# Four small moves and a new masked maximum in a transformer layer kernel: attention, soft mixture of experts, attention, soft mixture of experts

## The chip, the cores and the metric

The kernel runs on one core of one Trainium2 chip. The metric is device time in microseconds (us). The engines are TensorE (PE, with its weight loads as PEld), VectorE (DVE), ScalarE (ACT), GpSimd (POOL) and SyncE (SP, whose queue issues most DMAs). They run side by side and wait for one another by semaphores.

## What is computed

x has 4096 tokens of 256 numbers. It passes through four layers, each adding to x what it computes from the normalised x:

```python
x = x + attn_a(layernorm(x))     # 16 heads of 16, causal, denom = sum(exp) + exp(denom_bias)
x = x + ffn(layernorm(x))        # soft mixture of 64 experts with 32 slots each
x = x + attn_b(layernorm(x))     # 16 heads of 16, causal softmax
x = x + ffn(layernorm(x))        # the same weights again

# attention
sim = einsum('bhid,bhjd->bhij', q, k) / sqrt(16)
sim = where(j > i, -big, sim)
p = exp(sim - max_j(sim));  out = (p / sum(p)) @ v;  return out @ Wo.T

# mixture
logits = (x @ phi_w.T + phi_b).reshape(t, z, 64, 32)
D = softmax(logits, axis=slots);  C = softmax(logits, axis=experts)
X = D^T x;  X = tanh(layernorm(clip(X)));  Y = X @ expert_w + expert_b;  return C Y
```

## The kernel before, in words

The program is a row of stages, each with its own semaphores and a barrier of all engines at its end (`phase_of`): set-up, then for each of the two halves norm and projection (`norm_and_project`), attention, `project_out_and_norm`, `dispatch`, and `experts_and_combine`. The tags are set, a_qkv, a_att, f_in, f_disp, f_mix, b_qkv, b_att, g_in, g_disp, g_mix. A stage begins when the last engine of the one before has come to the barrier, so a DMA that SP waits for at the end of a stage holds up all engines.

**Set-up.** SP issues the loads of four weights and of x (eight groups), waits for GpSimd's memsets and selects, and then issues five copies: `x_rows` to DRAM (L150) and the turned halves of the mask and of the identity (L154). It waits for all of them at the stage's end (L155, L156).

**Norm and projection.** In layer a VectorE also folds and scales phi, the dispatch weights, in `area`. SP stores its high and low part to `phi_parts` in DRAM (L335) and waits for both stores. `project_out_and_norm` of each mixture loads phi from there.

**Attention.** Heads go in four quads of four. A unit is a quad and a group g of 512 queries; quads 0 and 2 take the groups upwards, quads 1 and 3 downwards, so there are 32 units a layer. Each unit first needs the row maxima of its scores, then the exponentials. For the maxima TensorE makes score items: one item is a pair of heads, one tile of 128 queries and one block c of up to 512 keys (`score`, L742). The two heads' matmuls use different rows of the array (r = 0 and 64) and different banks of PSUM. Where the block is the diagonal one (c == g) its width is 128, 256, 384 or 512 and its last 128 columns lie on the diagonal. There TensorE adds -3.0e38 above the diagonal with two further matmuls per head (L746, L747), each of 64 rows and 128 columns. VectorE takes both heads of an item in one reduction (L889). The ring of items holds two. The exponentials' scores are made the other way round, keys on partitions (`scores_t`, L778): four tiles a step, ScalarE's exp (L846) on each, then the products with V (`p_v`, L797). Which items are made behind which tile is a list worked out in advance (`ring_schedule`): the maxima run about a unit ahead of the exponentials, and behind tiles 1 and 3 of a step one item may stand, head 1 first and head 0 one tile on. In the descending quads the items become fewer towards the end.

**Dispatch.** 64 units (32 tiles of 128 tokens for each half of the slots). For each unit TensorE makes logits (L1105, 12 matmuls), VectorE two maxima and a subtraction (L1207 to L1212), ScalarE the exp, VectorE the sums and reciprocals, GpSimd the quotient d (L1185), ScalarE its high part (L1152), GpSimd its low part (L1189), and TensorE three tiles later the products with the tokens (L1117, 24 matmuls), gathered in four banks. In the second half, after every eighth tile, VectorE merges the two halves' maxima (L1219) and GpSimd cuts them into three bf16 parts (`cut_maxima`, four operations, L1173 to L1179); TensorE turns these three tiles later (L1126) and ScalarE keeps them (L1163). At the half and at the end ScalarE copies the four banks to xacc (L1157).

## Time and profile before

| | |
|---|---|
| Median of 3 runs | 4777.9 us (4777.64 to 4795.27) |
| The profiled execution | 4784.3 us, span 4782.5 us, mean granted TensorE clock 0.971 |
| TensorE busy | 4441.6 us, 93% |
| VectorE busy | 4075.7 us, 85% |
| ScalarE busy | 3132.5 us, 65% |
| GpSimd busy | 1211.5 us, 25% |
| Attention a from its first maximum to its last | 142.3 to 1506 us |

Times in the rows below are from the span's start. A busy share is an average over stages. In a timeline row the first number is the start, the second the length, and the brackets give how long the engine was idle before it and who released it. Rows of one shape are merged, and the number behind x is how many they hold. Matmuls are pipelined and their ends are modelled, so the length of a group of them is a little longer than the time it takes from the next.

### The profile page before, as it was taken

To read this page: it belongs to the slowest core of one execution; us is meant where nothing else is said; L and a number is where in the kernel's file an instruction comes from. 1 tells how busy PE (TensorE), PEld (TensorE's weight loads), DVE (VectorE), ACT (ScalarE), POOL (GpSimd) and SP (SyncE) were. 2 spreads that over 40 slices of the span, in tenths; PEclk is the share of its full clock that TensorE was granted. 3 is DMA by queue.
4 is the path that set the end of the run, shared out by engine and by line. 5 is a ranking of instruction groups with operands and counts; after the bars stand their busy time and mean duration, and the time that the engine had idled before them with its cause. 6 is when DMAs were issued, how large, how long until landed. Compare 5 with 4: busy or idle time off the path is not lost. (4 is left out here: it accounts for less than half of the span.)

```text
span 4782.5 us, 97694 instructions
## 1 busy us (share of the span) xinstructions
PE 4441.6 (93%) x40558; PEld 1955.9 (41%) x40558; DVE 4075.7 (85%) x4651; ACT 3132.5 (65%) x5879; POOL 1211.5 (25%) x1201
## 2 busy tenths in 40 slices
PE   7799999999998899899997999999999998998998
PEld 4222223222224566456662222232222345664666
DVE  5899998999885898678848999989998868885887
ACT  3378988889997444334344789888899974443443
POOL 1100001100002576445301000011000015774543
PEclk9799999999999899999997999999999999999999
DMA  6100000000000000310040000000000000004000
GB/s 183 54 21 2 2 15 15 14 14 4 2 2 23 1 1 1 107 36 0 0 126 26 17 2 2 22 9 15 15 2 2 2 22 1 1 1 142 10 13 13
DMA packets 73767, 112.29 MB, mean 23 GB/s; under 512 B 12501, under 2 KB 56789, under 8 KB 69077
## 3 DMA queue, kind: packets, MB, share of 16 engines
q1 hardware_dynamic: 68746, 99.96, 6.3%
q0 software_dynamic: 4608, 6.50, 1.0%
q8 instruction: 299, 4.90, 0.4%
q14 instruction: 114, 0.93, 0.1%
HBM read 73.70 MB, written 31.47 MB: 22 GB/s over the span
## 5 line engine op out<-in xcount | busy, mean ns | idle before, releaser
L889 DVE TENSOR_REDUCE b_att_mx<-ps 128x2 f32<-128x1024 f32 (+3 forms) x1152 | 1228.4, 1130 | 105.9 <-PE ps L742 80.6
L889 DVE TENSOR_REDUCE a_att_mx<-ps 128x2 f32<-128x1024 f32 (+3 forms) x1152 | 1227.9, 1130 | 102.3 <-PE ps L742 77.7
L846 ACT ACTIVATE b_att_pt<-ps 128x512 f32<-128x512 f32 (+3 forms) x2304 | 1146.9, 560 | 208.7 <-PE ps L778 179.0
L846 ACT ACTIVATE a_att_pt<-ps 128x512 f32<-128x512 f32 (+3 forms) x2304 | 1146.9, 560 | 207.2 <-PE ps L778 177.3
L797 PE MATMUL ps<-b_att_pt,b_v 128*17 128x256 f32 (+1 forms) x8704 | 672.6, 381 | 10.7 <-ACT b_att_osb L833 9.8
L797 PE MATMUL ps<-a_att_pt,a_v 128*17 128x256 f32 (+1 forms) x8704 | 670.5, 380 | 10.7 <-ACT a_att_osb L833 9.7
L723 POOL TENSOR_SCALAR_AFFINE_SELECT b_att_pt<-b_att_pt 128x512 f32<-128x512 f32 x128 | 81.4, 636 | 1122.9 <-ACT b_att_pt L846 1110.6
L723 POOL TENSOR_SCALAR_AFFINE_SELECT a_att_pt<-a_att_pt 128x512 f32<-128x512 f32 x128 | 81.4, 636 | 1120.4 <-ACT a_att_pt L846 1108.1
L778 PE MATMUL ps<-b_q,b_k 51*128 51x512 f16 (+3 forms) x1152 | 363.2, 370 | 0.2 <-ACT b_att_pt L846 0.2
L778 PE MATMUL ps<-a_q,a_k 51*128 51x512 f16 (+3 forms) x1152 | 361.3, 368 | 0.2 <-ACT a_att_pt L846 0.2
L742 PE MATMUL ps<-a_k,a_q 48*128 48x512 f16 (+3 forms) x1152 | 293.9, 379 | 51.9 <-DVE a_att_mx L889 37.9
L778 PE MATMUL ps<-b_att_q,b_att_k 51*128 51x512 f16 (+3 forms) x1152 | 338.7, 365 | 1.1 <-ACT b_att_pt L846 0.6
L778 PE MATMUL ps<-a_att_q,a_att_k 51*128 51x512 f16 (+3 forms) x1152 | 338.4, 365 | 1.0 <-ACT a_att_pt L846 0.6
L742 PE MATMUL ps<-b_k,b_q 48*128 48x512 f16 (+3 forms) x1152 | 298.0, 382 | 41.4 <-DVE b_att_mx L889 33.2
L742 PE MATMUL ps<-b_att_k,b_att_q 48*128 48x512 f16 (+3 forms) x1152 | 320.4, 365 | 5.1 <-DVE b_att_mx L889 4.8
L742 PE MATMUL ps<-a_att_k,a_att_q 48*128 48x512 f16 (+3 forms) x1152 | 320.3, 365 | 5.1 <-DVE a_att_mx L889 4.8
L1152 ACT CAST area<-area 128x1024 f16<-128x1024 f32 x128 | 133.8, 1045 | 287.7 <-POOL area L1185 287.7
L1189 POOL TENSOR_TENSOR area<-area 128x1024 f16<-128x1024 f32 x128 | 272.7, 2131 | 146.1 <-ACT area L1152 145.5
L797 PEld LDWEIGHTS ps<-b_att_pt,b_v 128*17 128x17 f32 x8704 | 145.2, 95 | 356.6 <-ACT b_att_pt L846 211.1
L797 PEld LDWEIGHTS ps<-a_att_pt,a_v 128*17 128x17 f32 x8704 | 145.1, 95 | 356.2 <-ACT a_att_pt L846 210.6
L1117 PE MATMUL ps<-f_xtok,area 128*128 128x256 f16 x1536 | 189.9, 283 | 26.5 <-POOL area L1189 22.7
L1117 PE MATMUL ps<-g_xtok,area 128*128 128x256 f16 x1536 | 190.2, 283 | 25.9 <-POOL area L1189 22.0
(319 smaller groups left out, 7241.0 us busy)
## 6 DMA issues: line engine op xcount, KB each, us to landing
f_mix_ct<-in_expert_w SPq DMA_DIRECT2D x64, 256.0 KB, 4.2
g_mix_ct<-in_expert_w SPq DMA_DIRECT2D x64, 256.0 KB, 4.3
a_parts_q<-a_qkv_cut SPq DMA_DIRECT2D x24, 256.0 KB
a_parts_k<-a_qkv_cut SPq DMA_DIRECT2D x24, 256.0 KB
b_parts_q<-b_qkv_cut SPq DMA_DIRECT2D x24, 256.0 KB
b_parts_k<-b_qkv_cut SPq DMA_DIRECT2D x24, 256.0 KB
x<-in_x SPq DMA_DIRECT2D x8, 512.0 KB, 8.6
out<-x SPq DMA_DIRECT2D x8, 512.0 KB, 2.9
```

Of the source, the lines that this page charges most:

```text
L723: pool.affine_select(out=block_p, in_=block_p, pattern=[[0, 4], [1, P]], compare_op=ALU.is_ge, fill=0.0, base=0, channel_multiplier=-1).th ...
L742: mm = pe.matmul(ps[:, at:at + width], q[quad % 2][h // 2][r:r + ROWS, t0:t0 + P], k[quad % 2][h // 2][r:r + ROWS, c * BANK:c * BANK + wid ...
L778: pe.matmul(ps[:, at:at + width], k[quad % 2][h // 2][r:r + ROWS_M, kb * P:(kb + 1) * P], q[quad % 2][h // 2][r:r + ROWS_M, (g + 1) * BANK ...
L797: mm = pe.matmul(OUT[32 * h:32 * h + VW, lo:hi], v[:, kb, 4 * quad + h, :], pt[:, s % PT_RING, h, lo - left:hi - left], start=(first and h ...
L846: act.activation(pt[:, s % PT_RING, i, 0:width], ps[:, at:at + width], ACT.Exp, scale=unscale).then_inc(pt_ready, 1)
L889: dve.tensor_reduce(mx[u % 2][:, h:h + 2, t, c], both, AX.X, ALU.max).then_inc(ring_read, 1)
L1117: mm = pe.matmul(ps[:, at:at + D], disp[:, n % DISP, dp, eb * P:(eb + 1) * P], xtok[:, t, xp, :], start=(t == 0 and i == 0 and eb % 2 == 0 ...
L1152: act.copy(disp[:, v % DISP, 0, :], ex[:, v % EX, :]).then_inc(high, 1)
L1189: pool.tensor_tensor(disp[:, n % DISP, 1, :], ex[:, n % EX, :], disp[:, n % DISP, 0, :], ALU.subtract).then_inc(d_ready, 1)
```

## The change

It has four parts.

1. Set-up: the five copies move from SP to the end of GpSimd's queue. SP still waits for them.
2. phi's stores: the projection of layer a no longer waits for them. Their semaphore is now kept for the whole kernel, and both mixtures wait for it before they load phi.
3. Dispatch: the four cutting operations no longer stand together between d and its low part, but one each behind the low parts of four tiles (all four behind the last tile for the last chunk). The turn comes six tiles after the chunk instead of three. The copies of the product banks each wait for their own bank (`xa_bank`) instead of for all.
4. Attention: for the diagonal items of quads 1 and 3 with g below 7 (`is_late`) the mask matmuls are left out. VectorE instead makes one `tensor_tensor_reduce` per head that adds a mask tile and takes the running maximum; the sum goes to a scrap tile. Before it VectorE waits until the previous such item is done. The mask tile is made by a memset and a copy at the start of the stage.

```diff
@@ set_up
-            sp.wait_ge(row_made, 2)
-            sp.dma_start(x_rows, ones_row[:, :, :]).then_inc(stored, 16)
-            sp.wait_ge(built, 2)
-            for turned, straight in ((m.mask_turned, m.mask_qk), (m.identb_turned, m.identb)):
-                for r in (0, P // 2):
-                    sp.dma_start(turned[r:r + P // 2, :], straight[P // 2 - r:P - r, :]).then_inc(turned_halves, 16)
             sp.wait_ge(turned_halves, 64)
             sp.wait_ge(stored, 16)
...
             pool.wait_ge(built, n)
+            pool.wait_ge(row_made, 2)
+            pool.dma_start(x_rows, ones_row[:, :, :]).then_inc(stored, 16)
+            for turned, straight in ((m.mask_turned, m.mask_qk), (m.identb_turned, m.identb)):
+                for r in (0, P // 2):
+                    pool.dma_start(turned[r:r + P // 2, :], straight[P // 2 - r:P - r, :]).then_inc(turned_halves, 16)
@@ norm_and_project
-                    sp.dma_start(early.phi_parts[part], parts[:, part, :, :]).then_inc(phi_stored, 16)
-                sp.wait_ge(phi_stored, 32)
+                    sp.dma_start(early.phi_parts[part], parts[:, part, :, :]).then_inc(early.phi_stored, 16)
@@ project_out_and_norm
+            sp.wait_ge(phi_stored, 32)
             for dst, src in loads:
                 sp.dma_start(dst, src).then_inc(loaded, 16)
@@ attention
+def is_late(u):
+
+    return any(UNITS[u][0] == quad and UNITS[u][1] < G - 1 for quad in (1, 3))
...
-                masked_end = c == g
+                masked_end = c == g and not is_late(u)
...
+            dve.memset(mask[:, 0:BANK - P], 0.0).then_inc(mask_made, 1)
+            dve.tensor_copy(mask[:, BANK - P:BANK], m.mask_qk[:, :]).then_inc(mask_made, 1)
+            dve.wait_ge(mask_made, 2)
...
+                if c == g and is_late(u):
+                    wait(dve, ring_read, dumped)
+                    dumped = n + 1
+                    for i in range(2):
+                        last = dve.tensor_tensor_reduce(dump[:, i, 0:width], both[:, i, :], mask[:, BANK - width:BANK], 1.0, NEG,
+                                                        ALU.add, ALU.max, mx[u % 2][:, h + i, t, c:c + 1])
+                    last.then_inc(ring_read, 1)
+                else:
+                    dve.tensor_reduce(mx[u % 2][:, h:h + 2, t, c], both, AX.X, ALU.max).then_inc(ring_read, 1)
@@ dispatch
-    TURN_AFTER = {min(n + 3, UNITS_D - 1 + LAG): j for n, j in CUT_AFTER.items()}
+    PIECES = 4
+    TURN_AFTER = {min(n + PIECES + 2, UNITS_D - 1 + LAG): j for n, j in CUT_AFTER.items()}
+    PIECE_AFTER = {n: [] for n in range(UNITS_D)}
+    for last_tile, j in CUT_AFTER.items():
+        for piece in range(PIECES):
+            PIECE_AFTER[min(last_tile + piece, UNITS_D - 1)].append((j, piece))
...
+                    if t == T - 1 and eb % 2 == 1 and eb + 1 < HALF_EB:
+                        mm.then_inc(xa_bank, 1)
...
-                    act.wait_ge(xa_ready, n - LAG + 1)
                     for b in range(HALF_EB // 2):
+                        if b + 1 < HALF_EB // 2:
+                            act.wait_ge(xa_bank, (HALF_EB // 2 - 1) * half + b + 1)
+                        else:
+                            act.wait_ge(xa_ready, n - LAG + 1)
...
-                if n in CUT_AFTER:
-                    cut_maxima(CUT_AFTER[n])
                 pool.wait_ge(high, n + 1)
                 pool.tensor_tensor(disp[:, n % DISP, 1, :], ex[:, n % EX, :], disp[:, n % DISP, 0, :],
                                    ALU.subtract).then_inc(d_ready, 1)
+                for j, piece in PIECE_AFTER[n]:
+                    cut_piece(j, piece)
```

## Rows read from the trace of the kernel before

**Rows 1.** Table of stretches of attention a: us, busy time of each engine (instructions), clock, DMA.
```profile
546.00:800.00 254.00, 247.54 (x2847) 75.01 (x2847) 239.11 (x252) 227.39 (x450) 17.68 (x49) 1.00 0.04 14
1205.00:1450.00 245.00, 239.08 (x2720) 72.00 (x2717) 210.53 (x213) 225.35 (x453) 15.29 (x38) 1.00 0.01 2
```
**Rows 2.** VectorE's groups by form, 546 to 800 us: busy us, mean ns | idle before.
```profile
L889 DVE TENSOR_REDUCE a_att_mx<-ps 128x2 f32<-128x1024 f32 x180 | 208.8, 1219 | 11.6 <-PE ps L742 10.7
...
L889 DVE TENSOR_REDUCE a_att_mx<-ps 128x2 f32<-128x256 f32 x15 | 6.3, 417 | 0.6 <-PE ps L747 0.6
```
**Rows 3.** VectorE's timeline: a full run of seven; behind a 128-wide and a 256-wide item.
```profile
568.60 8.00 DVE L889 TENSOR_REDUCE a_att_mx<-ps 128x2 f32<-128x1024 f32 x7
...
728.81 4.09 DVE L889 TENSOR_REDUCE a_att_mx<-ps 128x2 f32<-128x1024 f32 x4 [0.40 <-PE ps L742]
733.20 2.36 DVE L889 TENSOR_REDUCE a_att_mx<-ps 128x2 f32<-128x1024 f32 x2 [0.30 <-PE ps L742]
```
**Rows 4.** TensorE's timeline: products of P and V around an unmasked and a masked item.
```profile
1355.19 0.63 PE L797 MATMUL ps<-a_att_pt,a_v 128*17 128x256 f32 x8
...
1356.29 0.63 PE L797 MATMUL ps<-a_att_pt,a_v 128*17 128x256 f32 x8
...
1357.50 0.62 PE L797 MATMUL ps<-a_att_pt,a_v 128*17 128x256 f32 x8
```
**Rows 5.** Who SyncE's queue waited for in set-up: us in total, times, longest.
```profile
SPq L156 <- DMA x_rows<-set_ones_row: 3.7, 1, 3.7
```
**Rows 6.** Timeline of set-up and of GpSimd's first DMAs behind it.
```profile
12.72 0.31 POOL L178 TENSOR_SCALAR_AFFINE_SELECT sameneg<-sameneg 128x128 bf16<-128x128 bf16 x1
13.78 1.24 SPq L154 DMA_DIRECT2D identb_turned<-identb  x2
25.06 2.47 POOL L428 DMA_DIRECT2D a_k<-a_qkv_minus  x4 [0.31 <-POOL a_qkv_minus L425]
```
**Rows 7.** DMA issues: KB each, median us from issue to landing.
```profile
a_k<-a_qkv_minus POOLq DMA_DIRECT2D x4, 24.0 KB, 2.9
```
**Rows 8.** Who SyncE's queue waited for at the end of projection a.
```profile
SPq L73 <- DMA phi_parts<-area: 4.8, 1, 4.8
SPq L338 <- DMA a_parts_k<-a_qkv_cut: 1.7, 1, 1.7
```
**Rows 9.** Timeline there: phi's stores, and the exp of dbias in attention a.
```profile
130.49 1.11 SPq L335 DMA_DIRECT2D phi_parts<-area  x2
...
142.05 0.22 ACT L837 ACTIVATE a_att_dbias<-a_att_dbias 128x16 f32<-128x16 f32 x1 [0.74 <-DMA a_att_dbias<-in_a_db]
```
**Rows 10.** GpSimd's timeline at the first cut of dispatch f.
```profile
1820.29 2.13 POOL L1189 TENSOR_TENSOR area<-area 128x1024 f16<-128x1024 f32 x1 [1.21 <-ACT area L1152]
...
1829.77 1.91 POOL L1185 TENSOR_TENSOR area<-area,f_disp_rds 128x1024 f32<-128x1024 f32 x1
...
1834.07 2.12 POOL L1189 TENSOR_TENSOR area<-area 128x1024 f16<-128x1024 f32 x1
```
**Rows 11.** TensorE's timeline at the first and at the second cut of dispatch f.
```profile
1836.24 2.79 PE L1117 MATMUL ps<-f_xtok,area 128*128 128x256 f16 x24 [0.99 <-POOL area L1189]
...
1876.64 4.46 PE L1117 MATMUL ps<-f_xtok,area 128*128 128x256 f16 x24 [2.00 <-POOL area L1189]
```
**Rows 12.** Timeline at the half (first row) and at the end of dispatch f.
```profile
1792.78 2.05 ACT L1157 ACTIVATE f_xacc<-ps 128x512 f32<-128x512 f32 x4
...
1978.40 2.79 PE L1117 MATMUL ps<-f_xtok,area 128*128 128x256 f16 x24 [1.91 <-POOL area L1189]
...
1981.23 2.06 ACT L1157 ACTIVATE f_xacc<-ps 128x512 f32<-128x512 f32 x4 [6.25 <-PE ps L1117]
```
**Rows 13.** VectorE's groups by form: two inputs at 512 columns, and a very small operation.
```profile
L1010 DVE TENSOR_TENSOR f_xlnT<-ps,f_xlnT 128x512 f16<-128x512 f32 x8 | 5.5, 685 | 0.6 <-ACT f_xlnT L974 0.6
...
L458 DVE SCALAR_TENSOR_TENSOR a_qkv_cut<-ps,qk_scale,a_qkv_cut 128x512 f16<-128x512 f32 x32 | 23.4, 747 | 22.9 <-ACT a_qkv_cut L402 22.9
...
L213 DVE TENSOR_TENSOR qk_unscale<-set_wpower 128x2 f32<-128x2 f32 x1 | 0.1, 129 | 0.0
```

More of the change, by code:

```diff
@@ L632, in attention @@
         den, rden = sb("den", [P, KB, 4]), sb("rden", [P, KB, 4])
+        mask = sb("mask", [P, BANK], BF16)
+        dump = sb("dump", [P, 2, BANK], BF16)
         dbias = sb("dbias", [P, HEADS])
@@ L893, in _, with project_out_and_norm @@
                     dve.tensor_reduce(mfull[u % 2][:, :, :], mx[u % 2][:, :, :, 0:g + 1], AX.X, ALU.max).then_inc(m_full, 1)
[L897 removed]
+def project_out_and_norm(nc, m, ps, tag, attn, wo, bias, w, xlnT, by_token, loads, phi_stored):
     GT = 4
@@ L1167, in _, with cut_piece @@
         def _(pool):
-            def cut_maxima(j):
+            def cut_piece(j, piece):
                 parts = m3[j % 2]
-                pool.wait_ge(mc_made, j + 1)
-                wait(pool, c_turned, j - 1)
-                pool.tensor_copy(parts[:, :, 0, :], mc[:, :, :]).then_inc(c_chain, 1)
-                pool.wait_ge(c_chain, 3 * j + 1)
-                pool.tensor_tensor(mrest[:, :, :], mc[:, :, :], parts[:, :, 0, :], ALU.subtract).then_inc(c_chain, 1)
-                pool.wait_ge(c_chain, 3 * j + 2)
-                pool.tensor_copy(parts[:, :, 1, :], mrest[:, :, :]).then_inc(c_chain, 1)
-                pool.wait_ge(c_chain, 3 * j + 3)
-                pool.tensor_tensor(parts[:, :, 2, :], mrest[:, :, :], parts[:, :, 1, :], ALU.subtract).then_inc(c_cut, 1)
-                pool.wait_ge(c_cut, j + 1)
+                if piece == 0:
+                    pool.wait_ge(mc_made, j + 1)
+                    wait(pool, c_turned, j - 1)
+                    pool.tensor_copy(parts[:, :, 0, :], mc[:, :, :]).then_inc(c_chain, 1)
+                elif piece == 1:
+                    pool.wait_ge(c_chain, 3 * j + 1)
+                    pool.tensor_tensor(mrest[:, :, :], mc[:, :, :], parts[:, :, 0, :], ALU.subtract).then_inc(c_chain, 1)
+                elif piece == 2:
+                    pool.wait_ge(c_chain, 3 * j + 2)
+                    pool.tensor_copy(parts[:, :, 1, :], mrest[:, :, :]).then_inc(c_chain, 1)
+                else:
+                    pool.wait_ge(c_chain, 3 * j + 3)
+                    pool.tensor_tensor(parts[:, :, 2, :], mrest[:, :, :], parts[:, :, 1, :], ALU.subtract).then_inc(c_cut, 1)
             for n in range(UNITS_D):
@@ L1610, in mixture_layer @@
                 with nc.sbuf_tensor(f"{tag}_xtok", [P, T, 2, D], F16) as xtok:
-                    project_out_and_norm(nc, m, ps, f"{tag}_in", m.area, wo, bias, xacc[:, 0:DC, :], xlnT, xtok, loads)
+                    project_out_and_norm(nc, m, ps, f"{tag}_in", m.area, wo, bias, xacc[:, 0:DC, :], xlnT, xtok, loads, early.phi_stored)
                     dispatch(nc, m, ps, f"{tag}_disp", xtok, xlnT, phi, xacc, mct)
```

10 lines of the change are left out of this document (5 added, 5 removed).

## The prediction

> **What bounds the kernel now.** The busy shares (TensorE 93%, VectorE 85%) are averages over unlike stages, so the first view to read is the table of stretches, here for attention layer a [rows 1]. The reader is to see two regimes in it. While quad 1's maxima are made (546 to 800 us) TensorE is busy 247.5 us of 254 and VectorE 239.1: both are at their end, and VectorE has 14.9 us free. From 1205 us on, while quad 3's are made, up to 1450, VectorE has 34.5 us of 245 free, TensorE only 5.9. So the descending run of quad 3 is TensorE's; in quad 1's run the two take turns. The second view is VectorE's maxima by width and then in order of time [rows 2, 3], to price an item and to see where the idle time stands. The third is TensorE's order of work around a masked item [rows 4]. For the set-up and the end of the first projection I read who SyncE waited for and what was issued when [rows 5 to 9], and for the dispatch the order of GpSimd, TensorE and ScalarE around a cut, at the half and at the end [rows 10 to 12].
>
> **Set-up copies on GpSimd's queue.** Five copies leave SP and are issued by GpSimd after its last select. Today they stand on SP behind eight loads of x; the last is issued by 15.0 us (13.78 and 1.24), and SP then waits 3.7 us on x_rows and after it for the turned halves, so the stage ends not before 18.7 [rows 5, 6], and the next begins at 20.3. GpSimd's selects end at 13.03 (12.72 and 0.31); it issues four small DMAs in 2.47 us [rows 6], so five take 3.1, and with the 2.9 us to landing of its copies of minus [rows 7] they land at 19.0, on a queue of their own. SP's now end at about 19.5, as the barrier behind takes 0.8. What is then late is x itself, on whose queue nothing changes. I take -0.8 us, bounds -1.5 and +0.5 (if the two queues share the engines badly). Nothing is queued behind them on GpSimd in that stage. The Trainium skill, "DMA: Bandwidth & Descriptors", section on SWDGE and HWDGE, speaks against it: GpSimd's path has about 1 us to the first byte and SP's about 0.6. By that alone an estimate of the gain is 0.4 us less; no run here has shown the same copy on both.
>
> **phi's stores awaited by the mixture.** SP's last wait of the a projection is 4.8 us on phi_parts [rows 8], after the q and k parts have landed. It goes entirely. What is late next: dbias is the first DMA of attention a, and it is now issued while phi's two megabytes are still on that queue; VectorE's first maximum waits for the exp of dbias, which now runs from 142.05 to 142.27 [rows 9]. phi's issues end at 131.60, and with waits of 1.7 and 4.8 us [rows 8, 9] phi has landed at about 138.2. If dbias lands right behind phi, at 138.5 to 139.3, the exp ends at 138.8 to 139.6: a gain of 2.7 to 3.5 us. If dbias isn't held up, it is 4.8. I take -3.3, bounds -2.5 and -4.8. The new wait stands on SP in front of phi's loads of the mixture, 1.4 ms after the stores landed: nothing, in both layers.
>
> **Masks inside the maxima.** Per attention layer 14 units of quads 1 and 3 have 8 diagonal items each, 112 in all, 28 of each width. Each loses four 128-column mask matmuls on TensorE, and VectorE makes two reductions with a mask added instead of one over both heads.
> TensorE: the products of P and V recur after 1.10 us (1355.19 to 1356.29) with a full unmasked item between them, after 1.21 (to 1357.50) with a full masked one [rows 4]. Head 1's and head 0's matmuls lie on different rows of the array, so two of the four masks are already hidden: 0.11 us an item.
> VectorE: seven full items back to back take 8.00 us [rows 3], which is (8.00 - 1.22) / 6 = 1.130 from start to start. The forms [rows 2] give (1219 - 417) / 768 = 1.044 ns a column, so 0.061 us is fixed. Two operations instead of one cost one more 0.061. Each must also put out its running maximum. The trace has no such operation. From below that is nothing; from above it is a small operation of its own, 0.129 us (L213), the 0.061 us of overlap lost, and the 0.062 us by which a two-operator form exceeds a plain one at 512 columns (747 against 685) [rows 13], 0.25 in all. I take 0.13, the small operation, as the nearest row: 0.061 + 2 x 0.13 = 0.32 us more per item, ends 0.06 and 0.56. The Trainium skill, "VectorE: DVE Perf Modes", section "Two Vector instructions with no wait between them", says that an operation with an accumulator output is two instructions. By that the low end falls away and nothing else moves; no row of this trace has one.
> Quad 1's run: 56 x 0.32 = 17.9 us on an engine that has 14.9 us free. The free time stands behind the narrow items, where TensorE needs longer than VectorE: in the two rows at 728.81 and 733.20 [rows 3] 0.40 us behind a 128-wide and 0.30 behind a 256-wide one, 14 of each, so about 8.5 us are hidden there, and about 2 more in the last two units. 7 us stay, against which TensorE's saving counts for nothing, as VectorE is last. Ends: +1 and +21, and -2 if the idle gaps shrink with the masks.
> Quad 3's run: 56 x 0.11 = 6.2 us less on TensorE; the 17.9 us on VectorE lie in free time (34.5 us up to 1450 alone [rows 1]), but the ring is only two items deep, so I let 2 us through: -4, ends -6 and -1. VectorE's own memset and copy of the mask and the waits on earlier items cost under 0.5 us a layer; they lie behind the wait for dbias in layer a.
> Per layer 7 - 4 = +3, both +6; ends -16 and +40.
>
> **Dispatch lumps divided.** Around a cut TensorE stands still 2.00 us (here the second cut's row), then 0.99 (the first's) [rows 11]. The 2.00 comes from VectorE's merge of the two halves (L1219), through the reciprocals that GpSimd's product waits for; that merge isn't touched. The 0.99 comes from GpSimd's four cutting operations, which stand between the end of d at 1831.68 and the low part at 1834.07: 2.4 us [rows 10]. They lie between d and its low part, where GpSimd otherwise waits 1.21 us for ScalarE, so they cost it 1.2 net. Divided, they come behind the low part, where there is no wait to hide them: some 0.6 us each, on a round of 1.91, 1.21 and 2.13, 5.2 us, which is also what TensorE's 24 and 12 matmuls take. I followed GpSimd through the first cut by these durations: TensorE would wait 0, 0.36, 0.7 and 0.5 us, and the turn's own work and its wait for mct (0.4 and 0.7 us) are only moved three tiles on. The sum is 0.2 us worse at the first cut and 0.2 better at the next: 0 per cut, bounds -1 and +1, for six cuts.
> At the last tile the order does pay. Its low part starts at once, 1.24 us earlier, and TensorE's 1.91 us wait [rows 12] shrinks by that; the cut (2.4 us) lies beside the 2.6 us of products. The four copies of xacc, 2.06 us after the last product, start as each bank is ready, so that one and mct's 1.03 us are left: 1.3 us. Together -2.5 per dispatch, -5 for both, bounds -5.5 and -1.5 (the low level of the clock, below).
> At the half the freed banks change nothing: TensorE waits for the first copy of xacc, yet ScalarE only comes to it at 1792.78, with no idle time in front, straight behind its cast, which waited for GpSimd [rows 12]. It wasn't waiting for the products.
>
> **The sum** against the profiled execution: 4784.3 us (span 4782.5) - 0.8 - 3.3 + 6 - 5 + 0 = 4781. That execution is 6.4 us above the median of the runs shown, 4777.9, so the forecast is 4775.
>
> **The rivals.** *The masked maximum is much dearer* (slower): at 0.7 us an item more, quad 1's run exposes 56 x 0.7 - 10 = 29 us a layer and quad 3's saving is eaten by its two-deep ring; 58 - 9 = +49, 4827. It decides from about 0.55 an item, where the total passes +24. A form at half rate (1.044 ns more a column, 640 columns an item in the mean, 0.67 us) would give even 4871; the row for PSUM with a 16-bit SBUF operand, 685 ns for 512, speaks against that. 0.18.
> *TensorE alone bounds both descending runs* (faster): 224 x 0.11 = 24.6 us come off, plus 9.1 elsewhere: 4744. VectorE's 239.1 of 254 us in quad 1 speaks against it. 0.12.
> *The pieces also clear the stalls of the cuts*: 0.99 and 0.7 us at the first, the turn's waits and 1.67 us of low clock at the two later ones (24 products then take 4.46 us instead of 2.79 [rows 11, 12]), some 7 us a dispatch: 4761. The untouched 2.00 us stall in front of them speaks against it. 0.10.
>
> **How the numbers follow.** The forecast has 0.60, and with the third rival 0.70 is within 0.5%, 24 us, about what a measurement of this kernel can tell from no change. Faster 0.12, slower 0.18. The forecast's own bounds are 4745 and 4810 with every term at its end; as they don't all fall together I take 4757 below, and above I reach a little into the first rival, 4813.
>
> **What would show it.** The new maxima in the forms: 128 columns about 0.2, 512 about 0.6 to 0.7, with 0.1 to 0.15 of something behind each. TensorE without mask matmuls in the descending units, quad 3's run shorter by about 4 us, quad 1's longer by about 7. SP's 4.8 us wait gone, the first maximum 2.5 to 3.3 us earlier than the stage's order now gives. The 2.00 us stalls unchanged. Experts starting 2.5 us sooner after the last cut's unit. The prediction is wrong if the masked form runs at half rate, if quad 1's run gets shorter, or if stalls in the dispatch tip the clock to its lower level in other places than now.

## The result, and the profile after

The changed kernel takes 4756.2 us (median of 6 runs, 4752.22 to 4761.31), the kernel before on the same chip 4779.5 (6 runs, 4777.64 to 4795.27): a ratio of 0.9941, 95% interval 0.993 to 0.9952. The ratio makes it 28 us less; the medians are 23 apart. The forecast was 4775 within 4757 to 4813, so the time lies just below the range: the sign of the sum was right and its size was not, 3 us against 23 to 28. The profiled execution has a span of 4759.6 us (4782.5 before) at a mean clock of 0.973.

The stages' lengths, by the barriers between them, against before: projection a 9.2 us shorter, attention a 5.3 longer, its MoE input 0.9, dispatch f 8.1 and mixture f 2.7 shorter; attention b 4.2 and dispatch g 5.1 shorter, mixture g 1.9 longer, the rest within 0.3. Some of these differences are not the change's, since several places vary from one profiled kernel to the next where nothing was changed: the first maximum of attention a, the half and the second cut of a dispatch (all three below), units 0 to 7 of an attention (385.8 to 390.2 us over the 17 profiles of kernels here) and its units 16 to 23 (330.6 to 334.4). So attention a is longer only by 3.6 us in units 0 to 7, 3.2 in units 16 to 23 and 2.8 at its head, where dbias is late; its descending runs are 0.6 and 3.7 shorter.

In the descending runs TensorE has less to do and VectorE a little more. The table of stretches of the changed kernel answers [rows 1]; columns are us and the busy time of TensorE, its weight load, VectorE, ScalarE and GpSimd:
```profile
546.00:800.00 254.00, 246.52 (x2648) 65.18 (x2644) 243.36 (x417) 227.58 (x452) 18.78 (x53) 1.00 0.05 14
1205.00:1450.00 245.00, 238.19 (x2606) 65.21 (x2606) 214.37 (x326) 226.52 (x459) 16.05 (x39) 1.00 0.01 2
```
VectorE's groups by form from 546 to 800 us answer [rows 2, 13]: the masked maximum is one operation for each head, and behind it stands a read of the accumulator.
```profile
L906 DVE TENSOR_REDUCE a_att_mx<-ps 128x2 f32<-128x1024 f32 x166 | 193.2, 1218 | 8.4 <-PE ps L747 7.6
L902 DVE CUSTOM_DVE_ANT_0 a_att_dump<-ps,a_att_mask 128x512 bf16<-128x512 f32 x28 | 18.1, 683 | 0.3
...
L902 DVE CUSTOM_DVE_ANT_0 a_att_dump<-ps,a_att_mask 128x256 bf16<-128x256 f32 x28 | 10.7, 417 | 1.1 <-PE ps L747 1.0
L902 DVE DVE_READ_ACCUMULATOR2_ANT a_att_mx<- 128x1 f32 x110 | 9.1, 83 | 0.0
```
What an item costs is read not from these means but from start to start, in the order of time:
```profile
599.88 0.68 DVE L902 CUSTOM_DVE_ANT_0 a_att_dump<-ps,a_att_mask 128x512 bf16<-128x512 f32 x1
600.49 0.08 DVE L902 DVE_READ_ACCUMULATOR2_ANT a_att_mx<- 128x1 f32 x1
600.49 3.48 DVE L906 TENSOR_REDUCE a_att_mx<-ps 128x2 f32<-128x1024 f32 x3
...
734.18 0.55 DVE L902 CUSTOM_DVE_ANT_0 a_att_dump<-ps,a_att_mask 128x384 bf16<-128x384 f32 x1
734.65 0.08 DVE L902 DVE_READ_ACCUMULATOR2_ANT a_att_mx<- 128x1 f32 x1
734.65 0.55 DVE L902 CUSTOM_DVE_ANT_0 a_att_dump<-ps,a_att_mask 128x384 bf16<-128x384 f32 x1
```
From 599.88 to 600.49 are 0.61 us for one head at 512 columns. The read and the next operation have the same start: it lies wholly in the overlap, and the 83 ns cost nothing. Two heads are 1.22 us, where the plain item takes 1.130: 0.09 more, not 0.32.

The product of P and V around masked items in quad 3 answers [rows 4]. It recurs every 1.10 us, where it was 1.21:
```profile
1355.02 0.62 PE L802 MATMUL ps<-a_att_pt,a_v 128*17 128x256 f32 x8
...
1356.12 0.62 PE L802 MATMUL ps<-a_att_pt,a_v 128*17 128x256 f32 x8
...
1357.21 0.63 PE L802 MATMUL ps<-a_att_pt,a_v 128*17 128x256 f32 x8
```
TensorE's timeline at the first cut of dispatch f answers [rows 11]. The stall of 2.00 us is as before at this cut, and the 0.99 has become three small ones on the pieces, of which I had forecast 0.36, 0.7 and 0.5:
```profile
1822.40 2.79 PE L1140 MATMUL ps<-f_xtok,area 128*128 128x256 f16 x24 [2.00 <-POOL area L1218]
...
1833.17 2.79 PE L1140 MATMUL ps<-f_xtok,area 128*128 128x256 f16 x24 [0.17 <-POOL area L1218]
...
1839.01 2.79 PE L1140 MATMUL ps<-f_xtok,area 128*128 128x256 f16 x24 [0.46 <-POOL area L1218]
...
1844.55 2.79 PE L1140 MATMUL ps<-f_xtok,area 128*128 128x256 f16 x24 [0.16 <-POOL area L1218]
```
At the second and third cut the stall of 2.00 us has become 1.31, in both dispatches, though I had written that the merge behind it isn't touched:
```profile
1868.81 2.79 PE L1140 MATMUL ps<-f_xtok,area 128*128 128x256 f16 x24 [1.31 <-POOL area L1218]
```
And the head of attention b shows what I had put under half a microsecond, the copy of the mask:
```profile
2502.67 3.50 POOL L704 MEMSET b_att_minus<- 3x4096 f16 x1 [50.55 <-POOLq L76]
...
2503.51 2.72 DVE L859 COPY b_att_mask<-mask_qk 128x128 bf16<-128x128 bf16 x1
...
2506.26 1.02 DVE L906 TENSOR_REDUCE b_att_mx<-ps 128x2 f32<-128x256 f32 x2
```
The first maximum stands 4.0 us behind the stage's start (2502.3), where it was 1.0 (2518.7 behind 2517.7).

### The profile page after: what moved, and what is told of

Its sections match the earlier page's. It is cut to its first block and busy times, and to the rows that moved or that the text cites. A ratio compares the mean times of both kernels' runs of the same rounds, so it can differ in the third digit from the quotient of the medians.

```text
span 4759.6 us, 96793 instructions
## 1 busy us (share of the span) xinstructions
PE 4417.4 (93%) x39662; PEld 1902.1 (40%) x39662; DVE 4091.2 (86%) x5327; ACT 3128.1 (66%) x5879; POOL 1214.4 (26%) x1206
## 5 line engine op out<-in xcount | busy, mean ns | idle before, releaser
L906 DVE TENSOR_REDUCE a_att_mx<-ps 128x2 f32<-128x1024 f32 (+3 forms) x1040 | 1145.6, 1161 | 87.4 <-PE ps L747 74.7
L906 DVE TENSOR_REDUCE b_att_mx<-ps 128x2 f32<-128x1024 f32 (+3 forms) x1040 | 1145.0, 1161 | 82.3 <-PE ps L747 70.4
L747 PE MATMUL ps<-a_k,a_q 48*128 48x512 f16 (+3 forms) x1152 | 299.8, 385 | 47.2 <-DVE a_att_mx L906 37.8
L1140 PE MATMUL ps<-f_xtok,area 128*128 128x256 f16 x1536 | 183.8, 278 | 24.5 <-POOL area L1218 20.7
```

The costliest lines, as they stand in the source:

```text
L747: mm = pe.matmul(ps[:, at:at + width], q[quad % 2][h // 2][r:r + ROWS, t0:t0 + P], k[quad % 2][h // 2][r:r + ROWS, c * BANK:c * BANK + wid ...
L906: dve.tensor_reduce(mx[u % 2][:, h:h + 2, t, c], both, AX.X, ALU.max).then_inc(ring_read, 1)
L1140: mm = pe.matmul(ps[:, at:at + D], disp[:, n % DISP, dp, eb * P:(eb + 1) * P], xtok[:, t, xp, :], start=(t == 0 and i == 0 and eb % 2 == 0 ...
```

## The experiments

Lengths of units of attention go from ScalarE's first exp of a unit to that of the next (for the last unit to the end of its last exp), "eight units" of a dispatch from the maxima of unit 39, 47 or 55 to those eight later; a cut lies inside each. These lengths are of one profiled execution of each kernel, the ratios of all its executions. The end of a dispatch is from the last unit's maxima to TensorE's first matmul of the mixture. Ratios are to the kernel before, run beside them on the same chip.

**The four parts, each alone.** Each kernel is the kernel before with one part of the diff in the section on the change, here by its telling lines.

```diff
# only_masks: part 4
-                masked_end = c == g
+                masked_end = c == g and not is_late(u)
+                        last = dve.tensor_tensor_reduce(dump[:, i, 0:width], both[:, i, :], mask[:, BANK - width:BANK], 1.0, NEG,
+                                                        ALU.add, ALU.max, mx[u % 2][:, h + i, t, c:c + 1])
# only_dispatch: part 3
-                if n in CUT_AFTER:
-                    cut_maxima(CUT_AFTER[n])
+                for j, piece in PIECE_AFTER[n]:
+                    cut_piece(j, piece)
# only_phi: part 2
-                sp.wait_ge(phi_stored, 32)
# only_setup: part 1
-            sp.dma_start(x_rows, ones_row[:, :, :]).then_inc(stored, 16)
+            pool.dma_start(x_rows, ones_row[:, :, :]).then_inc(stored, 16)
```

> The kernel before with part 4 alone (mask matmuls out, masked maxima on VectorE, for the diagonal items of quads 1 and 3 below g = 7). Theory A, that a masked pair costs VectorE only 0.09 us more than the plain maximum because the running maximum's read-out overlaps the next operation: from the first maximum on, quad 1's run within 1 us of before, quad 3's run 3.7 us shorter, in both layers; against that the mask's copy at the stage's start delays the first maximum of layer b by 3 us and of layer a by about 1; together -3 to -6 us, apart from where the clock falls. Theory B, the recorded one (0.32 us more an item): quad 1's run 7 us longer, quad 3's 4 us shorter, +6 us in all. Theory C, that the masks count for nothing and attention b's gain is the clock's: both runs as before.

Measured: ratio 0.9986 (0.9977 to 0.9996), 6.7 us less. Units 8 to 15 are 0.6 us shorter and units 24 to 31 3.7 shorter, in both layers, and in the changed kernel the same to 0.1 us. The first maximum of b is 4.0 us behind the stage's start, 3.0 more than before; in a, where dbias lands early enough here, the mask's copy costs 0.8. Twice 4.3 off, 3.0 and 0.8 on make 4.8 us less, within the ratio's 2 to 11. The forecast's +7 in quad 1 is refuted; its -4 in quad 3 holds.

> The kernel before with part 3 alone (pieces, later turn, banks). Theory A: both dispatches are 5.5 us or more shorter, 3 of it behind the last unit, 1.3 at each of the second and third cut where the clock no longer falls, 0 at the first cut; together -11 to -14 us, more only if a half's stall meets no low clock. Theory B, the recorded one: -5 us, all of it at the end. Theory C, that the cuts' gain in the changed kernel came from other parts (another phase of the clock): the low stretches at the second and third cut are back here, and only the end's 3 us a dispatch stay.

Measured: 0.9967 (0.9954 to 0.998), 15.8 us less, more than the other three together. The eight units around the cuts take 47.1, 46.4 and 46.4 us in both dispatches, where before has 46.8, 47.7 and 47.7 (48.0 in g). The ends are 3.3 and 3.7 us shorter.

> The kernel before with part 2 alone (projection a doesn't wait for phi's stores). Theory A: the 4.8 us wait goes, dbias lands late behind phi and gives 1.5 to 2.3 us back, so the first maximum of layer a comes 2.5 to 3.3 us earlier; the further 3 us of the changed kernel there belong to another part or to chance in ScalarE's wait for a parts_q store. Theory B: the whole 6 us come from this part, ScalarE's wait for the store (8.0 us before, 5.2 in the changed kernel) included.

Measured: 0.9992 (0.9982 to 1.0002), 3.8 us less, though the interval reaches from 8.6 less to 1 more, so the time alone doesn't show a gain. SyncE's wait of 4.8 us [rows 8] is gone, and dbias is now what is late: ScalarE waits 2.2 us for it.

> The kernel before with part 1 alone (set-up copies issued by GpSimd). Theory A: the second stage starts within 0.5 us of before, because x's loads end the stage either way; total within 2 us. Theory B, the recorded one: it starts 0.8 us earlier. Theory C, that moving the copies off SP's queue shortens ScalarE's later wait for a parts_q store by 3 us: then the first maximum of layer a comes 3 us earlier here.

Measured: 0.9997 (0.9987 to 1.0006): nothing that can be told from zero. In the changed kernel SyncE's wait on x_rows is 6.8 us where it was 3.7 [rows 5], since it begins that much sooner, and the stage ends at 20.3 us where it ended at 20.0. But the profile of before has the shortest of the old set-ups: to the release of the barrier behind it, the eight kernels with the old set-up take 20.3 to 21.4 us, 20.9 in the mean, the seven with only the copies moved 20.3 to 20.7, 20.5 in the mean. That is 0.4 us earlier, not the 0.8 forecast.

The first maximum of attention a was at 146.4 us with only_setup and at 147.1 with only_masks, which in front of it adds only the copy's 0.8, against 142.3 before. What moves it most is a wait of ScalarE in the second half of projection a, for the store that still reads a buffer of a_qkv_cut. Waits from 90 to 160 us (us in total, times, longest), first of the changed kernel, then of only_setup:
```profile
ACT a_qkv_cut L400 <- DMA a_parts_q<-a_qkv_cut: 5.2, 1, 5.2
```
```profile
ACT a_qkv_cut L401 <- DMA a_parts_q<-a_qkv_cut: 11.8, 1, 11.8
```
It was 8.0 in the profile of before, 8.9 with only_phi, 10.8 with only_masks, and none with masks_kept below, whose first maximum came at 138.6. So 2.8 of the 6.1 us by which the changed kernel's first maximum is earlier are not the change's. Two kernels with the same wait show what is: late_turn (below; it has the old set-up and the old order of phi) waited 5.1 us and had its first maximum at 140.0, the changed kernel 5.2 and 136.2. That is 3.8 us for phi and set-up together, where 4.1 were forecast. It is one pair; three others with nearly equal waits (only_dispatch and merge_behind, before and copy_first, only_bank and after_again) give 4.4, 2.5 and 6.9. Why the store takes so unequally long I haven't tried.

**What a masked maximum costs, and what the masks cost TensorE.**

```diff
# masks_kept: the kernel before with the mask tile, and
+                if c == g and is_late(u):
+                    for i in range(2):
+                        last = dve.tensor_tensor_reduce(dump[:, i, 0:width], both[:, i, :], mask[:, BANK - width:BANK], 1.0, NEG,
+                                                        ALU.add, ALU.max, mx[u % 2][:, h + i, t, c:c + 1])
# no_masks: the kernel before, and
-                masked_end = c == g
+                masked_end = c == g and not is_late(u)
```

> The kernel before with the masked maxima alone on VectorE: TensorE still makes its mask matmuls in the descending runs, so the output has the mask added twice, and only VectorE's price is seen. Theory 'the masked form costs next to nothing' (0.09 us more than a plain item at 512 columns, 0.08 at 384, nothing at 128, as the changed kernel's trace reads): units 8 to 15 of each layer 0 to 2 us longer than before, units 24 to 31 0 to 1 us longer, the first maximum of layer b 3 us late for the mask's copy; +3 to +9 us in all. Rival 'the masked form costs the 0.32 us that was forecast, and TensorE's saved matmuls paid for it in the changed kernel': units 8 to 15 7 us or more longer, in all +15 to +25 us.

Measured: 1.0023 (1.0013 to 1.0033), 11 us more. Units 8 to 15 are 1.7 us longer in both layers and units 24 to 31 0.3 longer; with the 3 us at the head of b that is 7. The other 4 us I can't place: the profiled execution is the fastest of its ten (4781.1 us, median 4792.0). The price of the masked form is settled by the units' lengths: 1.7 us in quad 1, where the forecast had 7 left over.

> The kernel before with the masks of the descending runs left out on both engines: no mask matmuls and plain maxima, so that part of the computation is missing (the maxima run over future keys too), and only TensorE's saving is seen. Theory 'TensorE saves 0.11 us a masked item where it is last': units 24 to 31 4 to 6 us shorter than before in each layer; in units 8 to 15, where VectorE takes turns with it, 1 to 2 us shorter, close to the 0.7 of the changed kernel, and 10 to 15 us in all. Rival 'the saving in units 8 to 15 is as large as in the other run and VectorE's price ate it': 4 to 6 us shorter there too, some 20 us in all.

Measured: 0.9972 (0.9961 to 0.9983), 13 us less. Units 24 to 31 are 4.1 us shorter and units 8 to 15 3.0. Together with masks_kept these give -4.1 + 0.3 = -3.8 in quad 3, where the changed kernel shows -3.7, and -3.0 + 1.7 = -1.3 in quad 1, where it shows -0.6: there price and saving don't simply add, by 0.7 us. So in quad 1 TensorE's saving does count, against my step that VectorE is last there: both engines are, by turns.

**The end of the dispatch and the clock at the cuts.**

```diff
# only_bank: the kernel before, and on ScalarE, with xa_bank counted by TensorE behind each bank's last product
-                    act.wait_ge(xa_ready, n - LAG + 1)
+                        if b + 1 < HALF_EB // 2:
+                            act.wait_ge(xa_bank, (HALF_EB // 2 - 1) * half + b + 1)
+                        else:
+                            act.wait_ge(xa_ready, n - LAG + 1)
# late_turn: the kernel before, and
-    TURN_AFTER = {min(n + 3, UNITS_D - 1 + LAG): j for n, j in CUT_AFTER.items()}
+    TURN_AFTER = {min(n + 6, UNITS_D - 1 + LAG): j for n, j in CUT_AFTER.items()}
```

> The kernel before with one edit: the copies of xacc start when each bank is ready, not when all are. Theory 'only the last tile gains': three of four copies leave the path behind the last product, 1.3 to 1.6 us per dispatch; the gap between the half's last and next unit is as before (within 0.3 us apart from the clock), as ScalarE comes there late by itself. In all -2.6 to -3.2 us. Rival 'the whole 3 us of the changed kernel's dispatch end are the banks': -3 per dispatch. Second rival 'the half gains too': its pitch 1 us or more shorter at the full clock.

Measured: 0.999 (0.9981 to 1.0). The ends are 1.4 us shorter in both dispatches (1.3 was the step), and the half of g takes 11.74 us, as before (11.70). The banks are 1.4 of the 3.3 to 3.7 by which the ends of only_dispatch are shorter. TensorE's wait in front of the last products is 0.74 us there where it was 1.91 [rows 12]: the cut behind the low part gives 1.2, as forecast (1.24). Another 0.7 comes from the wait two products earlier, 1.71 us for 2.41, and in g 0.4 is the barrier's, which takes 0.8 us before and 0.4 here.

> The kernel before with one edit: the turn of a cut's masks stands three tiles later, while the cut itself is still one lump. Theory 'the pieces matter for the clock only by chance': the eight units around each cut take as long as before at the full clock (46.8 to 47.1 us), the 0.99 us stall behind the cut stays, and the end of the dispatch isn't earlier. Rival 'the turn standing right behind the 2.00 us stall is what let the clock fall at the second and third cut': no low stretch there in either dispatch, the second and third cut's eight units 1 to 1.3 us shorter, as in the changed kernel, with no piece divided.

Measured: 1.0011 (1.0001 to 1.002), 5 us more, so no gain as a whole, but in its profile the eight units around the second and third cut take 46.6 us in both dispatches, not 47.7: the stretch at the lower clock behind the stall is gone there, with no lump divided. TensorE at the second cut in late_turn, where before has 4.46 us for the same 24 products [rows 11], with a mean granted clock of 0.63 from 1876.6 to 1881.2 us, most of it at the lower level, 1.2 GHz:
```profile
1870.37 2.79 PE L1117 MATMUL ps<-f_xtok,area 128*128 128x256 f16 x24 [1.86 <-POOL area L1189]
...
1876.76 2.79 PE L1117 MATMUL ps<-f_xtok,area 128*128 128x256 f16 x24 [1.00 <-POOL area L1189]
```
How much of this is the edit's? Seven kernels here have cuts and turns as before (before, only_masks, only_phi, only_setup, masks_kept, no_masks, only_bank). In their 14 dispatches the third cut's eight units take 47.7 us or more every time, but the second cut's 47.7 in seven and 46.8 in the other seven. In the five profiles with the turn six tiles behind the cut and the merge in its old place (the changed kernel twice, only_dispatch, copy_first, late_turn) the 20 take 46.4 to 46.6. So the gain at the third cut goes with the later turn, and at the second it is half chance.

It isn't that the turn stands right behind the stall, as the rival had it. The slow products come first, at 1876.64 us, and the turn 5 us behind their end:
```profile
1886.15 0.61 PE L1126 MATMUL ps<-identb,f_disp_m 128*96 128x128 bf16 x8
```
What does differ in front of them in late_turn is that the turn of the cut before stands three tiles nearer, and that the stall is 1.86 us, not 2.00; in the changed kernel it is 1.31. Which of these keeps the clock up isn't shown. Nor does a stall of 2.00 us always bring it down: at the first cut and at half of the second ones it didn't. Against late_turn at the full clock the pieces with their shorter stall take 0.2 us off a cut (46.4 against 46.6).

And late_turn loses elsewhere. The end of dispatch g is 1.5 us longer (27.2 for 25.7), since its last three groups of products take 4.46, 4.28 and 4.46 us, where before has 4.38, 4.46 and 2.79. The rest of the loss I can't place: the profiled execution is the fastest of its ten (4776.8 us, median 4786.4).

The half varies too. Its step from unit to unit in dispatch f took 11.70 us before, 9.22 in the changed kernel, in only_masks and in late_turn, 10.87 in only_phi, 11.67 in a second run of the changed kernel, with the same 3.85 us wait each time; the products behind it ran now at one level of the clock, now at the other.

**What the stall of 2.00 us is.** In the kernel before it stands at three cuts of each dispatch; the changed kernel still has it at the first and 1.31 us at the other two. I took it for the work of VectorE's merge.

```diff
# merge_by_tile: the changed kernel, and in each unit from T on
-                    dve.tensor_tensor(mc[:, :, :], mcp[:, 0, tiles, :], mcp[:, 1, tiles, :], ALU.max).then_inc(mc_made, 1)
+                    dve.tensor_tensor(mc2[:, j % 2, i, :], mcp[:, 0, n - T, :], mcp[:, 1, n - T, :], ALU.max).then_inc(mc_made, 1)
# merge_and_half: that, and ScalarE at the half
+                    if n - LAG == T - 1:
+                        for b in range(3):
+                            keep_bank(0, b)
# best: that, and the mask in the set-up
+            dve.tensor_copy(m.mask_wide[:, BANK - P:BANK], m.mask_qk[:, :]).then_inc(w_chain, 1)
```

> The changed kernel once more, on the chip and in the rounds of the three below, so that they can be held against it. 4752 to 4762 us, ratio to before 0.993 to 0.996. Theory 'the early part varies by chance': the first maximum of attention a may move by several us with ScalarE's wait on the store of a_parts_q (0 to 12 us in the runs so far), while units 8 to 15 (329.1 us) and 24 to 31 (305.4 and 305.7 us) and the dispatch's eight units (47.1, 46.4, 46.4 us) stay within 0.3 us. Rival 'the changed kernel gained there': the wait stays near 5.2 us and the first maximum near 136.

Measured: 0.9948 (0.9931 to 0.9964), 4760.2 us. ScalarE's wait was 10.1 us and the first maximum came at 141.0, while units 8 to 15 and 24 to 31 and the cuts' eight units are the same to 0.1 us.

> The changed kernel with the merge of the two halves of the cut's maxima made tile by tile on VectorE, right behind each tile, not in one operation in front of the cut. Theory 'the 2.00 us stall in front of each cut is that merge, which holds up the reciprocals': the stall goes at all three cuts in the middle of each dispatch, the eight units around a cut take 44.5 to 45.5 us, not 46.4 or 47.1, and the kernel is 8 to 13 us faster than the changed one (4743 to 4749). Rival 'VectorE's own four passes over a tile (4 x 1.21 us and 0.35 of a pitch of 5.21) are the bound, so eight small merges cost what the one did': the eight units within 0.5 us, total within 4 us.

Measured: 0.9969 (0.9957 to 0.998), 8 us slower than the changed kernel beside it, and the eight units take 47.8, 47.2 and 47.2 us. The theory falls. Why, the timeline shows, here with GpSimd's line beside VectorE's:
```profile
1816.73 2.13 POOL L1218 TENSOR_TENSOR area<-area 128x1024 f16<-128x1024 f32 x1 [1.21 <-ACT area L1177]
1817.31 1.59 DVE L1250 TENSOR_TENSOR f_disp_mc<-f_disp_mcp 128x32 f32<-128x32 f32 x1
...
1823.67 0.18 DVE L1250 TENSOR_TENSOR f_disp_mc<-f_disp_mcp 128x32 f32<-128x32 f32 x1
```
The same 32 columns take 0.18 us or 1.59. The long one begins while GpSimd's low part runs and ends at 1818.90, when that has ended (1818.86). So it is with all 64 of them: the 18 that begin while GpSimd is in an operation take 1.42 us or more and end 0.04 to 0.06 us behind it, and the 46 others take 0.18. In the kernel before the merge of 256 columns does the same, beside the first row of [rows 10], which ends at 1822.42:
```profile
1820.88 1.83 DVE L1219 TENSOR_TENSOR f_disp_mc<-f_disp_mcp 128x256 f32<-128x256 f32 x1
```
It isn't work but waiting: it ends at 1822.71, 0.29 us behind GpSimd. The mask's copy is another: it ends at 2506.23, GpSimd's memset at 2506.17. The Trainium skill has this in "SBUF — State Buffer", section "SBUF: two separate sides": the port pair that VectorE and GpSimd share is locked for a whole instruction, and whichever comes second blocks; on VectorE's side it names operations with two SBUF inputs (against a GpSimd operation that reads SBUF) and those in a 2-port mode. These rows agree for a VectorE operation with two operands in SBUF (1.59 for 0.18 us); for the copy from SBUF to SBUF they show the wait, but no row tells its mode. VectorE's passes that read PSUM, and its sum over area, which has one input, keep their 1.21 us beside the same GpSimd operations.

This also tells why the stall at the second and third cut shrank. In the changed kernel the second cut's merge begins 1.28 us into GpSimd's low part and takes 1.13 us; in the kernel before it begins 0.59 us into it and takes 1.83. That is the 0.7 us between 2.00 and 1.31, and it is the same 0.7 at the last cut, in front of the dispatch's end.

> As merge_by_tile, and at the half ScalarE copies the first three banks of xacc before it makes the last tile's last step, since the banks are ready then. Theory 'TensorE waits at the half for the first copy, which stands behind ScalarE's own cast': the wait of 3.85 us at the half shrinks by 2 to 3.5 us, at the high clock the pitch there falls from 9.22 to 6 to 7.5 us; 4 to 8 us for both dispatches. Rival 'the last bank decides': pitch within 0.6 us of 9.22.

Measured: 0.9949 (0.9933 to 0.9966), 10 us less than merge_by_tile. The step at the half is 6.70 us in both dispatches, whatever the clock did before.

> As merge_and_half, with the mask tile of the maxima made once in the set-up, not by VectorE's memset and copy at the head of each attention (2.72 us for the copy there). Theory 'the copy holds up the first maximum of attention b by 3 us and is hidden in a behind dbias': first maximum of b 1.0 us behind the stage's start, not 4.0, 3 us less in all. Rival 'something else is late there, the minus columns of GpSimd': within 1 us of the kernel without it.

Measured: 0.9953 (0.9936 to 0.9969), not apart from the kernel without it. The first maximum of b stands 1.0 us behind the stage's start and the stage is 2.8 us shorter; the rest of the difference is in the places that vary.

**The order against GpSimd alone.**

```diff
# merge_behind: the changed kernel, and
+                if n > 0:
+                    sums(n - 1)
                 if n in CUT_AFTER:
                     ...
                     dve.tensor_tensor(mc[:, :, :], mcp[:, 0, tiles, :], mcp[:, 1, tiles, :], ALU.max).then_inc(mc_made, 1)
-                if n > 0:
-                    sums(n - 1)
# copy_first: the changed kernel, and on GpSimd at the head of attention
+            pool.wait_ge(mask_made, 2)
             pool.memset(minus[:, :], -1.0 / M_SCALE).then_inc(set_up, 1)
```

> The changed kernel with one edit: VectorE merges the two halves of the cut's maxima behind the sum and reciprocal of the unit before, not in front of them. Theory 'the merge is held up by GpSimd's running product' (it lasts 1.83 us in the trace of before, from 1820.88 to 1822.71, and GpSimd's low part ends at 1822.42): behind the reciprocal GpSimd is about done, the merge takes 0.3 to 0.6 us, the 2.00 us stall in front of each middle cut goes or falls under 0.5, the eight units around a cut take 44.4 to 45.2 us in place of 47.1 and 46.4, and the kernel is 8 to 12 us faster than the changed one. Rival 'the merge is slow by itself': 1.8 us wherever it stands, and it then delays the next unit's maxima; eight units within 0.6 us of 46.4. Second rival 'the merge then holds up GpSimd's next product': as long as before, with GpSimd waiting in its place.

Measured: 0.9932 (0.9919 to 0.9946); 4752.9 us, 7 less than the changed kernel's 4760.2 of the run before and 3 less than its 4756.2, so as a whole not apart from it (the ratios' intervals overlap), and not the 8 to 12 us expected. The eight units take 45.4 us around nearly every cut (45.6 once) and TensorE's 2.00 us in front of it have become 0.25. VectorE's merge in three kernels, from the groups by form of dispatch f, before, changed and merge_behind:
```profile
L1219 DVE TENSOR_TENSOR f_disp_mc<-f_disp_mcp 128x256 f32<-128x256 f32 x4 | 7.3, 1826 | 0.0
```
```profile
L1250 DVE TENSOR_TENSOR f_disp_mc<-f_disp_mcp 128x256 f32<-128x256 f32 x4 | 5.2, 1303 | 0.0
```
```profile
L1252 DVE TENSOR_TENSOR f_disp_mc<-f_disp_mcp 128x256 f32<-128x256 f32 x4 | 1.5, 377 | 0.1
```
1826 ns became 377 by a change of place alone. Neither rival holds: it isn't slow by itself, and GpSimd's next product isn't held up. The gain per dispatch is 1.7 + 1.0 + 1.0 = 3.7 us, somewhat under the 4 to 6 that were expected.

> The changed kernel with one edit: GpSimd's memset of minus at the head of each attention waits until VectorE's copy of the mask is made. Theory 'the copy (2.72 us, 2503.51 to 2506.23) is held up until GpSimd's memset (2502.67 to 2506.17) ends': it takes under 0.3 us, the first maximum of layer b comes 1.0 to 1.5 us behind the start of its stage, not 4.0, and layer b gains 2.5 to 3 us; in a nothing changes, as dbias is waited for. Rival 'the copy is slow by itself': 2.7 us still, and the minus columns 3.5 us later.

Measured: 0.9942 (0.9927 to 0.9957), the changed kernel's time within the interval. But the head of b is as expected; GpSimd's memset now begins behind the copy:
```profile
2502.71 0.13 DVE L860 COPY b_att_mask<-mask_qk 128x128 bf16<-128x128 bf16 x1
2502.88 1.02 DVE L907 TENSOR_REDUCE b_att_mx<-ps 128x2 f32<-128x256 f32 x2
2502.90 3.50 POOL L705 MEMSET b_att_minus<- 3x4096 f16 x1 [51.57 <-DVE b_att_mask L860]
```
The copy takes 0.13 us, not 2.72, and the first maximum stands 1.4 us behind the stage's start. Its 2.6 us don't show in the total, whose executions lie 14 us apart; in this profile units 16 to 23 of b, which vary as said, took 3.4 us more.

> The changed kernel with merge_behind's order, with the first three banks of xacc copied at the half before the last tile's last step, and with the mask made once in the set-up. Theory 'the three gains add up': 8 to 12 us from the cuts, 4 to 9 from the two halves (pitch 6.7 in place of 9.22 and 11.8), 3 from layer b: 4733 to 4745 us. Rival 'what one gives the clock's low stretches or another engine take': under 10 us in all.

Measured: 0.9904 (0.9889 to 0.9919), 4738.2 us (4 runs, 4734.26 to 4741.29), 47 us less than before beside it and the fastest of all. The eight units take 45.4 us, the halves 7.1, the first maximum of b comes 0.9 us behind the stage's start (2491.2, 2490.3). The sum that was expected holds.

## Why the prediction was too high

**Masks, forecast +6, measured -5.7 (in the changed kernel's profile, twice 4.4 off and 3.0 on): the step that failed.** The prediction put 0.32 us more on a masked item: 0.061 for one more operation and 0.13 for each running maximum. The first half is right, the second isn't: the read of the accumulator takes 83 ns and lies in the overlap with what follows, so two operations cost 0.09 more than one at 512 columns, near the low end of 0.06. The sum had 0.32 for it. (That an operation with an accumulator output is two instructions, as the prediction cited from the Trainium skill, the trace agrees with; that this makes it dearer than the low end is true of 0.03 us.) At 0.09 quad 1 would have got at most 56 x 0.09 = 5 us, less than the gaps I had counted as 8.5. masks_kept shows 1.7 for it, so not all of it is hidden. Having taken the nearest row for an operation that the trace didn't show, I should have asked not how long it lasts but whether it lies between two starts. Quad 3 came out at -3.7 for -4. And in quad 1 TensorE's saving is worth 3.0 us (no_masks), where I had counted nothing, as the sum was made for one last engine in a stretch where two take turns.

**The mask's own preparation, forecast under 0.5 us a layer, is 3.0 in b.** In a of the changed kernel it hides behind dbias, which is late there; in only_masks it costs 0.8. The copy is held up by GpSimd's memset, which stood in the trace of before at the same place; I had costed it by its size.

**Dispatch, forecast -5, measured -12 in only_dispatch's profile and -16 by its ratio.** What the sum counted was right: the banks gave 1.4 (1.3 forecast) and the cut behind the last low part 1.2 (1.24). Two steps failed. The first is "that merge isn't touched": its place against GpSimd's low part moved, and 0.7 us less of waiting at three of the four cuts of a dispatch is 4.2 us in both. The pieces cost 0.3 us at the first cut, where 0.2 was forecast; with the shorter stall the second and third are 0.4 faster at the full clock. The second is the clock, which the sum put at nothing: 0.9 us at each second cut and 0.9 and 1.2 at the third ones against the profile of before, of which the second cut's comes and goes by chance. The third rival had this in its price, with a chance of 0.10, because the stall in front is untouched. At 4761 us it lay nearer to the measured 4756 than the forecast did. That the clock stays up with the later turn is measured; why it does stays open.

**Phi, forecast -3.3, measured -3.8 alone, and set-up, forecast -0.8, measured nothing by the ratio and 0.4 in the stage's mean**, both within their bounds, though the intervals of both include zero. What is late next is what was named, dbias. For set-up the working itself gave 19.0 us against 19.5, half a microsecond and not 0.8.

**The sum by what was measured**: 0 - 3.8 - 5.7 - 11.8 = -21.3 (the last from the lengths of only_dispatch's two dispatches: 2.2 + 3.3 and 2.5 + 3.7), to -28 by the four ratios (1.4 + 3.8 + 6.7 + 15.8). The medians differ by 23 and, in the ratio, 28. So nothing here shows the parts hindering one another.

**The rivals.** That TensorE alone bounds both descending runs would have given 24.6 us less; no_masks shows 7.1 a layer, 14 in both: a little over half of it. A dearer maximum is out: masks_kept is 11 us slower, where 0.7 us an item would have made 58.

**The range.** Its low end of 4757 held the masks' range badly: with -16 as the end of that term and the third rival's -14 the cases reached far lower, and I let them count for too little together. The upper sum was wrong as well: with every term at its end it is 4820, not 4810; nothing hangs on that here.

## What to carry to other kernels

Cost an operation that the trace doesn't show by what it adds between two starts, with the overlap of its neighbours as the first candidate for the answer, and not by the length of a similar row. Where a short VectorE operation between two SBUF tensors stands in front of something late, look at what GpSimd is doing at that moment; if it ends when GpSimd's operation ends, move it, don't divide it: here that gave 1.7 us at a first cut, where dividing it cost 8 us in all. Before a stretch at the lower clock is put down to an edit, look at the same place in kernels without the edit, and at what comes first: half of the second cuts had none with nothing changed. And where two engines take turns, ask both for the price and the saving, by a kernel that has the one without the other.

## What the chip showed that was not expected

- The accumulator's read stands in the trace with 83 ns and costs no time between back-to-back operations (0.61 us from start to start for an operation of 0.68).
- A VectorE merge of 32 columns takes 0.18 us or 1.59, one of 256 columns 0.38 or 1.83, and a copy of 128 columns 0.13 or 2.72, by whether GpSimd is in the middle of an operation.
- The first maximum of attention a moves between 134.8 and 147.9 us over the kernels here, with ScalarE's wait on one store between 0 and 11.8. That is over a quarter of a per cent of the whole, more than some of the parts studied here; its cause stays open.
